# One PSUM bank for each half of the turned weights in the causal stage of a six-layer attention kernel

## The chip, the cores and the metric

The kernel runs on one core of one Trainium2 chip. The metric is the device time of one execution in microseconds, the median of several runs. TensorE (PE) does the matmuls and the transposes through the identity and writes only to PSUM. VectorE (DVE) and ScalarE (ACT) read PSUM and do the arithmetic element by element. GpSimd (POOL) works in SBUF alone here, and SyncE (SP) starts the transfers. PSUM is used as eight banks of 128 x 512 numbers.

## The reference

Input `x` is 8 sequences of 512 tokens with 256 features, all float32. Six layers follow each other, each over all eight sequences: attention "a" (8 heads, low-rank keys and values), two feed-forward layers "f" with local attention, the causal attention "b", and again the two "f" layers with the same weights. What the change touches is "b":

```python
qkv = x @ w_qkv + b_qkv                       # x is layer-normed; 16 heads of 16
dot = jnp.einsum('bhid,bhjd->bhij', q, k)
q_norm_sq = jnp.sum(q * q, axis=-1, keepdims=True)
k_norm_sq = jnp.sum(k * k, axis=-1, keepdims=True)
vals = q_norm_sq + k_norm_sq.transpose(0, 1, 3, 2)
scores = dot * dot / (vals - 2.0 * dot + EPSILON) * SCORE_SCALE
mask = jnp.triu(jnp.ones((Lq, Lq), dtype=scores.dtype), k=1) * -1000000000.0
attn = jax.nn.softmax(scores + mask[None, None, :, :], axis=-1)
out = jnp.einsum('bhij,bhjd->bhid', attn, v)
out = out.transpose(0, 2, 1, 3).reshape(Bq, Lq, E)
return out @ w_out + b_out
```

## The kernel before, in words

Everything stays in SBUF. The work is cut into 48 units `u`: layer `u // 8`, sequence `u % 8`. The causal layer is units 24 to 31. A unit's work is cut into parts, each named by a kind, a unit and an index, and each kind belongs to one engine.

A causal unit has 24 steps: 8 pairs of heads times three groups of rows of the score matrix (`B_TILES`: row tiles 1 and 0, then tile 2, then tile 3, of 128 rows each). Only the blocks at or below the diagonal are computed, 3, 3 or 4 blocks of 128 x 128 for each of the two heads. One step is this chain:

- PE `bden` and `bdot`: the denominator and the dot product, each into a pair of banks (`wide0`, `wide1` or `wide2`, one bank for each head). In the trace they are the matmuls `wide<-hid` and `wide<-x,w_up`, and `bden` ends with `wide<-far_b,ident_b`.
- ACT `bnum` (square of the dot product, L1249) and `bguess` (logarithm and exponential for a first reciprocal, L1260 and L1264).
- DVE `bclose` (L1422) and `bmul` (L1430 and the four or two instructions of L1436): one Newton step for the reciprocal, the scores, and the largest of each row. POOL `neg` changes that to the bias of the exponential (L1655).
- ACT `exp` (L1287).
- PE `turn_a` and `turn_b`: 6 or 8 transposes of 128 x 128 (L896) into PSUM, two to four of them in each half. The halves are called the turned weights here.
- The copies to SBUF: of half a by ACT (`pt_a`, L1294) in the first of three steps and by DVE (`pt_c`, L1471) in the others, and of half b by DVE (`pt_b`), where the blocks on the diagonal are multiplied by the causal mask (L1479) and the rest is copied (L1482).
- PE `mix`: the product with the values, into `o_ps`. After 24 steps follow `sel`, `fan` and the output projection `proj` on PE, with `osum` and `out_b` (L1496) and `res` (L1502) on DVE between and behind them.

The next unit's head of the work (`bqkv` on PE, `row` on DVE at L1409, `bk` and `bq` on PE) is woven between the steps.

Seven of the eight banks are handed out by name; `o_ps` is the eighth. `wide0` to `wide2` are banks 0 to 5 in pairs, and bank 6 is `turn_ps`. In the causal stage before the change, `bk`, `bq`, `sel` and `fan` use bank 6, and the two halves of the turned weights share one pair: half a lies in its first bank, half b in its second. `turn_a` takes the pair, and whoever is given that pair next waits for the copies of both halves.

What sets the order is a planner that runs when the kernel is built. `ordered()` walks through all parts with the durations of `cost()`, and for each engine takes, among the parts that could start no later than `PATIENCE` after the first possible one, the part with the smallest due time. A due time is the part's place in its unit plus an offset from the table `DUE`. `rooms()` says which banks a part may use, `buffer_at()` picks among them the one that is free first by the planner's durations, and `readers_of()` says whose end frees them. The engines then run their lists in that order. Each part waits on semaphores for what it needs; a PE part also waits in `psum_read()` for the readers of the earlier contents of its banks.

Of the kernel before, what the change touches and what calls it, by code (L numbers as in the profile page):

```python
# [13 lines left out]
P = 128  # L14
# [50 lines left out]
B_OWN = [4, 2, 2]  # L65
# [148 lines left out]
def normed_before(u):  # L214
# [244 lines left out]
def holder_of(part):  # L459

    kind, u, i = part
    if kind == "turn_b" and stage_of(u) == "b":
        return ("turn_a", u, i)
    return (kind, u, 0) if kind in ("proj", "down") else part
# [6 lines left out]
def rooms(part):  # L471


    kind, u, i = part
    st = stage_of(u)
    pairs, single = [(f"wide{k}", (2 * k, 2 * k + 1)) for k in range(3)], (f"bank{BANKS - 1}", (BANKS - 1,))
    if st == "a" and kind in ("score", "turn_a", "turn_b"):
        return [single] + [(f"bank{k}", (k,)) for k in range(A_PAIRS * 2, BANKS - 1)]
    if kind in NARROW and not (kind == "turn_a" and st == "b"):
        return [single]  # L480
    return pairs[:A_PAIRS] if st == "a" else pairs


def readers_of(part):

    kind, u, i = part
    last = [(r, u, 0 if kind in ("proj", "down") else i) for r in READERS[kind]]
    if kind == "turn_a" and stage_of(u) == "b":
        last.append(("pt_b", u, i))
    if kind == "score" and stage_of(u) == "f":  # L490
        last.remove(("exp", u, i))
    return last
HOP = 0.2

PATIENCE = 0.263


def ordered():
# [34 lines left out]
    def buffer_at(part):  # L533
# [5 lines left out]
        for name, banks in rooms(part):  # L539
            at = 0.0  # L540
            for holder in {holders[k] for k in banks} - {None}:
                for r in readers_of(holder):
                    if r in parts:
                        at = max(at, end[r] + HOP) if at is not None and r in end else None
            if at is not None and (best is None or at < best[0]):
                best = (at, name)
# [81 lines left out]
def build(nc, d):  # L628
    stack = ExitStack()
    with stack:  # L630
# [128 lines left out]
        def psum_read(pe, part):  # L759
# [36 lines left out]
            elif kind == "turn_a" and stage_of(u) == "b":  # L796
                pe.wait_ge(S[first_copy(u, i)], nth(first_copy(u, i), u, i))
                pe.wait_ge(S["pt_b"], nth("pt_b", u, i))
            elif kind == "turn_a":
                pe.wait_ge(S["pt_a"], nth("pt_a", u, i))  # L800
# [88 lines left out]
        def tensor_program(eng):  # L889
# [9 lines left out]
            for part in ORDER["PE"]:  # L899
# [139 lines left out]
                elif kind in ("turn_a", "turn_b") and stage_of(u) == "b":  # L1039
                    pe.wait_ge(S["exp"], nth("exp", u, i))  # L1040
                    for k, block in B_TURNS[i % 3][kind == "turn_b"]:
                        to, at = turned_to(i, k, block), k * b_width(i) + block * P
# [280 lines left out]
        def vector_program(eng):  # L1323
# [10 lines left out]
            for part in ORDER["DVE"]:  # L1334
# [132 lines left out]
                elif kind == "pt_c":  # L1467
# [3 lines left out]
                    eng.tensor_copy(prob_t[SLOTS[u, i]["pt"]][:, 0:w], wide[PLACE["turn_a", u, i]][:, 0:w]).then_inc(S["pt_c"], 1)  # L1471
                elif kind == "pt_b":
# [3 lines left out]
                    if stage_of(u) == "b":  # L1476
                        dve.wait_ge(S["const"], 16 * 3)
                        ps, met, n = wide[PLACE["turn_b", u, i]], P * B_OWN[i % 3], P * len(B_TURNS[i % 3][1])
                        last = eng.tensor_tensor(blocks(pt[:, 512:512 + met]), blocks(ps[:, 512:512 + met]),  # L1479
                                                 causal_keep[:, :].unsqueeze(1).to_broadcast([P, met // P, P]), ALU.mult)  # L1480
                        if n > met:
                            last = eng.tensor_copy(pt[:, 512 + met:512 + n], ps[:, 512 + met:512 + n])  # L1482
# [395 lines left out]
```

## Time and profile before

| | us |
|---|---|
| median of 3 runs | 4371.79 (4367.45 to 4373.05) |
| profiled execution, time | 4363.23 |
| profiled execution, span | 4361.2 |
| PE busy | 4070.3 (93%) |
| DVE busy | 3157.0 (72%) |
| ACT busy | 2469.0 (57%) |
| causal stage, taken as 1981 to 3010 us | 1029 |
| one causal unit | 133.4 |

Busy time is a share of the span, an average over stages. The table by stretches shows that PE is nearly always busy in the "f" stages and that DVE is the busiest engine in the causal stage. "PEclk" is the share of the full TensorE clock that was granted. Idle time of an instruction stands in brackets with the engine and the line that ended it. "PEld" is the weight load ahead of a matmul, which overlaps the matmul before it.

### The profile page before, as it was taken

To read this page: it belongs to the slowest core of one execution; us is meant where nothing else is said; L and a number is where in the kernel's file an instruction comes from. 1 tells how busy PE (TensorE), PEld (TensorE's weight loads), DVE (VectorE), ACT (ScalarE), POOL (GpSimd) and SP (SyncE) were. 2 spreads that over 40 slices of the span, in tenths; PEclk is the share of its full clock that TensorE was granted. 3 is DMA by queue.
4 is the path that set the end of the run, shared out by engine and by line. 5 is a ranking of instruction groups with operands and counts; after the bars stand their busy time and mean duration, and the time that the engine had idled before them with its cause. 6 is when DMAs were issued, how large, how long until landed. Compare 5 with 4: busy or idle time off the path is not lost.

```text
span 4361.2 us, 66411 instructions
## 1 busy us (share of the span) xinstructions
PE 4070.3 (93%) x23504; PEld 2586.4 (59%) x23504; DVE 3157.0 (72%) x7625; ACT 2469.0 (57%) x5353; POOL 1763.7 (40%) x2051
## 2 busy tenths in 40 slices
PE   8999999999999999988888888888999999999997
PEld 4666556666666666655555555555666666666664
DVE  6667677777667667658988889888777676677663
ACT  5556554454454545439887788875544544544441
POOL 2223365555546556420111110014555565565551
PEclk9999999999999999998998889989999999999999
DMA  2000000000010000000000000101000000100000
GB/s 78 11 16 6 25 11 6 3 3 6 23 30 11 13 8 8 26 19 20 23 23 20 20 24 23 37 20 33 4 6 3 3 26 8 35 15 18 13 20 22
DMA packets 63176, 78.38 MB, mean 18 GB/s; under 512 B 15312, under 2 KB 47616, under 8 KB 62848
## 3 DMA queue, kind: packets, MB, share of 16 engines
q1 hardware_dynamic: 62848, 74.14, 5.9%
q8 instruction: 189, 3.10, 0.3%
q14 instruction: 139, 1.14, 0.1%
HBM read 36.39 MB, written 12.58 MB: 11 GB/s over the span
## 4 chain that ended last, share of the span: by engine, by line
PE 70%; DVE 14%; ACT 10%; issue 5%; DMA 0%; SPq 0%; POOL 0%; DVEq 0%; ACTq 0%
PE wide L893 48%; PE o_ps L893 8%; PE wide L896 7%; PE turn_ps L896 5%; ACT prob L1270 3%; DVE w_up L1422 2%; PE turn_ps L893 2%; DVE prob L1436 1%; DVE hid L1430 1%; ACT prob L1287 1%; DVE turned L1368 1%; ACT x L1260 1%; ACT hid L1260 1%; DVE ss L1375 1%; DVE turned L1382 1%
## 5 line engine op out<-in xcount | busy, mean ns | idle before, releaser
L893 PE MATMUL wide<-x,w_up 128*128 128x512 f32 (+3 forms) x2528 | 837.5, 540 | 4.2 <-DVE x L1533 2.2
L893 PE MATMUL wide<-w_in,x_t 128*128 128x512 f32 (+2 forms) x1920 | 801.4, 561 | 4.6 <-ACT x_t L1183 1.3
L1661 POOL TENSOR_SCALAR prob<-prob,st 128x256 f32<-128x256 f32 (+1 forms) x1024 | 554.4, 560 | 577.2 <-DVE st L1460 576.6
L1270 ACT ACTIVATE prob<-prob,st 128x256 f32<-128x256 f32 (+1 forms) x1024 | 479.5, 470 | 166.9 <-DVE st L1447 166.5
L893 PEld LDWEIGHTS wide<-x,w_up 128*128 128x128 f32 (+2 forms) x2528 | 374.9, 192 | 300.4 <-issue 283.3
L893 PEld LDWEIGHTS wide<-w_in,x_t 128*128 128x128 f32 x1920 | 339.3, 191 | 332.4 <-issue 323.0
L893 PE MATMUL o_ps<-pt,v 128*32 128x128 f32 (+2 forms) x5120 | 485.1, 332 | 37.8 <-DVE pt L1486 30.6
L1633 POOL TENSOR_TENSOR rn<-ss,minus_half 128x16 f32<-128x16 f32 x128 | 433.7, 3389 | 126.2 <-DVE ss L1377 121.9
L893 PEld LDWEIGHTS o_ps<-pt,v 128*64 128x64 f32 (+1 forms) x5120 | 308.2, 128 | 219.4 <-issue 89.7
L1447 DVE CUSTOM_DVE_ANT_0 prob<-wide,local_mask 128x256 f32<-128x256 f32 (+1 forms) x1024 | 335.3, 382 | 140.4 <-PE wide L893 140.4
L1625 POOL TENSOR_TENSOR sines<-raw,rot 128x512 f32<-128x512 f32 x256 | 351.5, 1394 | 196.7 <-ACT raw L1190 196.7
L1298 ACT ACTIVATE o_t<-o_ps 128x512 f32<-128x512 f32 x192 | 113.5, 591 | 490.3 <-PE o_ps L893 490.3
L1655 POOL TENSOR_SCALAR st<-st 128x2 f32<-128x2 f32 (+1 forms) x192 | 39.8, 207 | 858.8 <-DVE st L1436 858.8
L893 PE MATMUL wide<-k_t,q_t 64*128 64x256 f32 (+2 forms) x2450 | 366.4, 411 | 2.2 <-ACT turned L1193 1.2
L893 PE MATMUL wide<-w_out,o_t 128*128 128x256 f32 x1536 | 351.3, 388 | 1.9 <-ACT o_t L1298 1.9
L893 PE MATMUL wide<-hid 18*128 18x256 f32 x992 | 204.1, 507 | 148.9 <-DVE pt L1479 99.5
L893 PE MATMUL wide<-w_down,hid 128*128 128x256 f32 (+1 forms) x1536 | 330.5, 383 | 4.6 <-DVE hid L1556 4.6
L896 PEld LDWEIGHTS turn_ps<-ident,prob 128*128 128x128 f32 x1932 | 230.5, 141 | 175.6 <-issue 139.5
L893 PEld LDWEIGHTS wide<-w_out,o_t 128*128 128x128 f32 x1536 | 298.7, 196 | 58.1 <-issue 14.2
L896 PE MATMUL turn_ps<-ident,prob 128*128 128x128 f32 x1932 | 310.2, 278 | 24.2 <-ACT pt L1294 14.8
L1556 DVE SCALAR_TENSOR_TENSOR hid<-wide,bias_up,hid 128x512 f32<-128x512 f32 (+1 forms) x224 | 144.8, 669 | 241.6 <-ACT hid L1317 122.6
L896 PE MATMUL wide<-ident,prob 128*128 128x128 f32 x1828 | 272.3, 294 | 13.5 <-DVE raw L1409 11.0
(166 smaller groups left out, 7498.9 us busy)
## 6 DMA issues: line engine op xcount, KB each, us to landing
kept<-resid SPq DMA_DIRECT2D x16, 512.0 KB, 2.6
x<-kept SPq DMA_DIRECT2D x16, 512.0 KB, 3.3
w_up<-hid SPq DMA_DIRECT2D x62, 128.0 KB, 2.2
x<-hid SPq DMA_DIRECT2D x62, 128.0 KB, 2.3
shifted<-resid SPq DMA_DIRECT2D x32, 224.0 KB
w_in<-in_f_wqkv SPq DMA_DIRECT2D x4, 1536.0 KB, 6.5
w_up<-in_f_w SPq DMA_DIRECT2D x4, 1492.0 KB, 6.5
resid<-in_x SPq DMA_DIRECT2D x8, 512.0 KB, 7.9
```

What stands on the lines that cost most here:

```text
L893: return eng.matmul(out, lhsT, rhs, start=start, stop=stop, skip_group_check=True)
L896: return eng.transpose(out, in_, ident[:, :])
L1260: last = eng.activation(inv[:, k * w:(k + 1) * w], ps[:, 512 * k:512 * k + w], ACT.Ln, bias=guess_add[s][:, i % 3, h:h + 1])
L1270: last = eng.activation(pr[:, local_span(t)], pr[:, local_span(t)], ACT.Exp, bias=sm[:, t:t + 1], scale=-1.0, accum_out=sm[:, 4 + t:5 + t])
L1287: last = eng.activation(pr[:, side], pr[:, side], ACT.Exp, bias=sm[:, c:c + 1])
L1298: eng.activation(o_t[:, i, :], o_ps[:, :], ACT.Copy).then_inc(S["out"], 1)
L1422: eng.scalar_tensor_tensor(out=two(den, slice(0, w)), in0=two(ps[:, :], slice(0, w)), scalar=DEN_MIN, in1=two(inv, slice(0, w)), op0=ALU.m ...
L1447: eng.tensor_tensor_reduce(pr[:, local_span(t)], ps[:, local_span(t)], local_mask[:, P if t == 0 else 0:256], -1.0, LOW, ALU.add, ALU.min, ...
L1556: last = eng.scalar_tensor_tensor(out=hid[rows, m, cols], in0=ps[rows, 512 * k + cols.start:512 * k + cols.stop], scalar=bias_up[rows, m:m ...
L1625: last = eng.tensor_tensor(halves(sines[(o - 1) % 2][:, side]), halves(r[:, side])[:, :, ::-1, :], rot[:, 2 * z + 1, i, :].rearrange("p (u ...
L1633: eng.tensor_tensor(rn[(o - 1) % 2][:, 0:16], ss[(o - 1) % 2][:, 0, :], minus_half[:, 0:16], ALU.pow).then_inc(S["rn"], 1)
L1661: last = eng.tensor_scalar(pr[:, local_span(t)], pr[:, local_span(t)], sm[:, 8 + t:9 + t], 1.0, ALU.mult, ALU.mult)
```

## The change

In the causal stage each half of the turned weights becomes a tile of its own with a single bank. `rooms()` lists bank 6 first and then banks 5 down to 0, and the planner takes the first that is free. A half's bank is given back by the half's own copy. `buffer_at()` counts a bank as free no earlier than PE itself is, so that among banks that are free by then the first of the list is taken. The transposes of half b are written to columns 0 and up of its bank, and the copies read from there. Since `bk`, `bq`, `sel` and `fan` still use bank 6 alone, they now share it with the halves. No instruction is added or removed.

The offsets of the causal kinds in `DUE` are other numbers, and `PATIENCE` goes from 0.263 to 0.318. The table holds only offsets of the due times; two of its lines stand here. `PATIENCE` applies to all stages.

```diff
-    ("b", "turn_a"): -0.01, ("b", "pt_c"): -0.015, ("b", "mix"): 0.031, ("b", "sel"): 0.017, ("b", "osum"): 0.179,
+    ("b", "pt_c"): -0.012, ("b", "mix"): 0.031, ("b", "sel"): 0.017, ("b", "bn_h"): 0.005, ("b", "turn_b"): -0.12,
...
@@ holder_of(part)
     kind, u, i = part
-    if kind == "turn_b" and stage_of(u) == "b":
-        return ("turn_a", u, i)
     return (kind, u, 0) if kind in ("proj", "down") else part
@@ rooms(part)
-    if kind in NARROW and not (kind == "turn_a" and st == "b"):
+    if st == "b" and kind in ("turn_a", "turn_b"):
+        return [single] + [(f"bank{k}", (k,)) for k in reversed(range(BANKS - 1))]
+    if kind in NARROW:
         return [single]
@@ readers_of(part)
-    if kind == "turn_a" and stage_of(u) == "b":
-        last.append(("pt_b", u, i))
...
-PATIENCE = 0.263
+PATIENCE = 0.318
@@ buffer_at(part)
+            if at is not None and stage_of(u) == "b":
+                at = max(at, free_at["PE"])
@@ psum_read(pe, part)
-            elif kind == "turn_a" and stage_of(u) == "b":
+            elif kind == "turn_a":
                 pe.wait_ge(S[first_copy(u, i)], nth(first_copy(u, i), u, i))
-                pe.wait_ge(S["pt_b"], nth("pt_b", u, i))
-            elif kind == "turn_a":
-                pe.wait_ge(S["pt_a"], nth("pt_a", u, i))
@@ tensor_program
-                        to, at = turned_to(i, k, block), k * b_width(i) + block * P
+                        to, at = turned_to(i, k, block) % 512, k * b_width(i) + block * P
@@ vector_program, pt_b
-                        ps, met, n = wide[PLACE["turn_b", u, i]], P * B_OWN[i % 3], P * len(B_TURNS[i % 3][1])
+                        ps, met, n = buffers[PLACE["turn_b", u, i]], P * B_OWN[i % 3], P * len(B_TURNS[i % 3][1])
-                        last = eng.tensor_tensor(blocks(pt[:, 512:512 + met]), blocks(ps[:, 512:512 + met]),
+                        last = eng.tensor_tensor(blocks(pt[:, 512:512 + met]), blocks(ps[:, 0:met]),
```

Below, `wide0` to `wide2` are the pairs and `turn_ps` is bank 6. The first place is on PE at the seam of two causal units, units 27 and 28, where step 0 of unit 28 is done and step 1 follows. `wide<-w_in,x_t` is the next unit's `bqkv`, `<-ident,prob1` x6 are the halves of step 21 of unit 27, `<-ident,k_t0` is `bk`, and `<-hid`, `<-x_2,w_up` and `<-far_b` are step 1's `bden` and `bdot`. Before:

```order
L893 MATMUL wide1<-w_in,x_t 128x512
L893 MATMUL wide1<-w_in,x_t 128x256
L896 MATMUL wide0<-ident,prob1 128x128 x6
L896 MATMUL turn_ps<-ident,k_t0 128x128 x4
L893 MATMUL wide1<-hid 128x384 x2
L893 MATMUL wide0<-x_2,w_up 128x384 x2
L893 MATMUL wide1<-far_b,ident_b 128x128 x2
L896 MATMUL wide2<-ident,prob2 128x128 x6
```

After, from the turning of half b of step 21 (`prob1`, four blocks) through step 0's `bden` and `bdot` (256 and 128 columns), half a of step 21 (two blocks), the halves of step 22 (`prob2`) and step 1's `bden` and `bdot` (384 columns):

```order
L896 MATMUL turn_ps<-ident,prob1 128x128 x4
L893 MATMUL wide1<-hid 128x256 x2
L893 MATMUL wide2<-x_2,w_up 128x256 x2
L893 MATMUL wide1<-hid 128x128 x2
L893 MATMUL wide2<-x_2,w_up 128x128 x2
L893 MATMUL wide1<-far_b,ident_b 128x256 x2
L896 MATMUL turn_ps<-ident,prob1 128x128 x2
L893 MATMUL o_ps<-pt0,v1 32x128 x8
L896 MATMUL wide2<-ident,prob2 128x128 x2
L896 MATMUL turn_ps<-ident,prob2 128x128 x4
L893 MATMUL wide0<-hid 128x384 x2
L893 MATMUL wide2<-x_2,w_up 128x384 x2
```

Step 1's `bdot` took the pair that both halves of step 21 had just filled; now step 21's halves lie in bank 6, one after the other, and step 1's `bden` and `bdot` take pairs 0 and 2, where pair 2 holds only half b of step 22. `bqkv` stands further ahead and no longer before these rows.

The second place is on PE at the head of unit 28. `<-w_in,x_t` is the second `bqkv` of unit 29, `turn_ps<-o_t,w_down` is `sel`, `<-ident,prob1` is step 1 turned, and the 384 columns are step 4. Before:

```order
L893 MATMUL wide1<-w_in,x_t 128x512
L893 MATMUL wide1<-w_in,x_t 128x256
L893 MATMUL turn_ps<-o_t,w_down 32x512 x4
L893 MATMUL wide0<-hid 128x384 x2
L893 MATMUL wide2<-x_2,w_up 128x384 x2
L893 MATMUL wide0<-far_b,ident_b 128x128 x2
L896 MATMUL wide1<-ident,prob1 128x128 x6
```

After:

```order
L893 MATMUL wide2<-hid 128x384 x2
L893 MATMUL wide0<-x_2,w_up 128x384 x2
L893 MATMUL wide2<-far_b,ident_b 128x128 x2
L893 MATMUL turn_ps<-o_t,w_down 32x512 x4
L896 MATMUL wide0<-ident,prob1 128x128 x2
L893 MATMUL wide1<-w_in,x_t 128x512
L893 MATMUL wide1<-w_in,x_t 128x256
...
L896 MATMUL wide2<-ident,prob1 128x128 x4
```

Before, the halves of step 1 went into pair 1 right where `bqkv` had been; now half b goes ahead of `bqkv`, half a behind it, and both into banks that `bqkv` does not hold.

The third place is on DVE at the same seam. L1341, L1345 and L1328 are the layer norm statistics of a later unit, L1409 is `row`, L1479 with 512 columns is `pt_b` of step 21, and L1422 is `bclose`. Before:

```order
L1436 ISA st3 128x1
L1341 BN_STATS stat_h<-resid 128x6 x4
L1345 BN_AGGR stat_h<-stat_h 128x2 x4
L1328 TENSOR_SCALAR stat_h<-stat_h 128x4
L1409 TENSOR_TENSOR raw0<-wide1,w_in 128x768
L1479 TENSOR_TENSOR pt1<-wide0,causal_keep 128x512
L1422 SCALAR_TENSOR_TENSOR w_up<-wide2,x_2 128x768
```

After:

```order
L1479 TENSOR_TENSOR pt1<-turn_ps,causal_keep 128x256
L1409 TENSOR_TENSOR raw0<-wide2,w_in 128x768
L1471 COPY pt1<-wide1 128x512
L1471 COPY pt0<-turn_ps 128x512
L1479 TENSOR_TENSOR pt0<-wide1,causal_keep 128x256
L1482 COPY pt0<-wide1 128x256
L1341 BN_STATS stat_h<-resid 128x6 x4
L1345 BN_AGGR stat_h<-stat_h 128x2 x4
L1328 TENSOR_SCALAR stat_h<-stat_h 128x4
L1479 TENSOR_TENSOR pt1<-turn_ps,causal_keep 128x512
L1422 SCALAR_TENSOR_TENSOR w_up<-wide0,hid 128x1024
```

The statistics still stand right before `pt_b` of step 21, but `row` and the copies of steps 19 and 20 stand before them, and `bclose` and `bmul` of step 23 (prob3, 512 columns for each head) now come behind that copy.

## Rows read from the trace of the kernel before

**Rows 1.** The page: span, and busy time, share and instructions of each engine.
```profile
span 4361.2 us, 66411 instructions
PE 4070.3 (93%) x23504; PEld 2586.4 (59%) x23504; DVE 3157.0 (72%) x7625; ACT 2469.0 (57%) x5353; POOL 1763.7 (40%) x2051
```

**Rows 2.** Busy time by stretches: eight "f" units, then the causal stage.
```profile
core 0: us, PE busy (x) PEld busy (x) DVE busy (x) ACT busy (x) POOL busy (x), PEclk, DMA share, GB/s
646.00:1312.00 666.00, 657.24 (x3268) 420.43 (x3266) 467.55 (x1217) 325.11 (x777) 371.34 (x377) 1.00 0.04 12
1981.00:3010.00 1029.00, 855.45 (x7042) 550.24 (x7040) 901.63 (x1955) 851.27 (x1493) 131.69 (x349) 0.90 0.09 22
```

**Rows 3.** The same for two causal units.
```profile
2216.00:2349.40 133.40, 111.55 (x905) 71.90 (x905) 115.40 (x252) 108.99 (x194) 14.44 (x47) 0.88 0.08 21
2349.40:2482.80 133.40, 111.52 (x905) 71.76 (x905) 115.42 (x252) 108.89 (x194) 14.46 (x47) 0.88 0.08 21
```

**Rows 4.** Groups of the causal stage, 1981 to 3010 us; last, idle before and releaser.
```profile
L893 PE MATMUL wide<-hid 18*128 18x256 f32 x976 | 198.7, 502 | 148.8 <-DVE pt L1479 99.5 <-DVE pt L1482 27.1 <-DVE pt L1471 9.3
L1249 ACT ACTIVATE prob<-wide 128x768 f32<-128x768 f32 x183 | 159.9, 874 | 89.6 <-PE wide L893 78.5 <-remote 9.0
L1422 DVE SCALAR_TENSOR_TENSOR w_up<-wide,x 128x768 f32<-128x768 f32 x122 | 116.0, 951 | 13.6 <-ACT x L1264 12.1
L1471 DVE COPY pt<-wide 128x512 f32<-128x512 f32 x125 | 85.7, 686 | 13.9 <-PE wide L896 13.9
L1422 DVE SCALAR_TENSOR_TENSOR w_up<-wide,hid 128x1024 f32<-128x1024 f32 x62 | 75.7, 1221 | 22.2 <-ACT hid L1264 22.2
L1496 DVE TENSOR_TENSOR o_t<-turn_ps,o_t 128x512 f32<-128x512 f32 x29 | 20.0, 691 | 31.6 <-PE turn_ps L893 31.6
```

**Rows 5.** PE at the seam of units 27 and 28, in order of time.
```profile
2440.54 0.60 PE L896 MATMUL turn_ps<-ident,k_t 128*128 128x128 f32 x4
2444.47 1.01 PE L893 MATMUL wide<-hid 18*128 18x384 f32 x2 [3.33 <-DVE pt L1479]
```

**Rows 6.** DVE and ACT at the same seam, in order of time.
```profile
2443.64 0.68 DVE L1479 TENSOR_TENSOR pt<-wide,causal_keep 128x512 f32<-128x512 f32 x1
2448.85 0.96 DVE L1422 SCALAR_TENSOR_TENSOR w_up<-wide,x 128x768 f32<-128x768 f32 x1 [0.48 <-ACT x L1264]
2452.06 0.69 DVE L1471 COPY pt<-wide 128x512 f32<-128x512 f32 x1 [0.18 <-PE wide L896]
2454.74 1.22 DVE L1422 SCALAR_TENSOR_TENSOR w_up<-wide,hid 128x1024 f32<-128x1024 f32 x1 [1.33 <-ACT hid L1264]
...
2446.19 0.81 ACT L1249 ACTIVATE prob<-wide 128x768 f32<-128x768 f32 x1 [2.90 <-PE wide L893]
```

**Rows 7.** PE at the head of unit 28, in order of time.
```profile
2461.26 0.29 PE L893 MATMUL wide<-far_b,ident_b 128*128 128x128 bf16 x2
2463.66 1.06 PE L896 MATMUL wide<-ident,prob 128*128 128x128 f32 x6 [2.11 <-DVE raw L1409]
```

**Rows 8.** Busy time by stretches around that wait, and one unit earlier.
```profile
2463.00:2464.00 1.00, 0.34 (x3) 0.34 (x4) 1.00 (x2) 0.97 (x3) 0.01 (x1) 1.00 0.00 0
2464.00:2485.00 21.00, 21.00 (x86) 11.77 (x85) 12.76 (x22) 10.13 (x18) 1.74 (x7) 0.51 0.06 13
2331.00:2352.00 21.00, 21.00 (x85) 11.88 (x84) 12.93 (x23) 9.86 (x18) 1.74 (x7) 0.51 0.06 13
```

**Rows 9.** An "f" unit: PE in order of time, then ACT.
```profile
921.94 8.75 PE L893 MATMUL wide<-x,w_up 128*128 128x512 f32 x20
930.52 0.49 PE L896 MATMUL turn_ps<-ident,prob 128*128 128x128 f32 x3
977.81 1.74 PE L893 MATMUL o_ps<-pt,v 128*64 128x256 f32 x16 [1.10 <-DVE pt L1486]
...
926.22 0.19 ACT L1270 ACTIVATION_READ_ACCUMULATOR prob<-prob,st 128x1 f32 x1
931.92 0.60 ACT L1202 ACTIVATE q_t<-wide 128x512 f32<-128x512 f32 x1 [5.51 <-PE wide L896]
```

More of the change, by code:

```diff
@@ L1470, in vector_program @@
                     w = P * len(B_TURNS[i % 3][0])
-                    eng.tensor_copy(prob_t[SLOTS[u, i]["pt"]][:, 0:w], wide[PLACE["turn_a", u, i]][:, 0:w]).then_inc(S["pt_c"], 1)
+                    eng.tensor_copy(prob_t[SLOTS[u, i]["pt"]][:, 0:w], buffers[PLACE["turn_a", u, i]][:, 0:w]).then_inc(S["pt_c"], 1)
                 elif kind == "pt_b":
@@ L1477, in vector_program @@
                         dve.wait_ge(S["const"], 16 * 3)
-                        ps, met, n = wide[PLACE["turn_b", u, i]], P * B_OWN[i % 3], P * len(B_TURNS[i % 3][1])
-                        last = eng.tensor_tensor(blocks(pt[:, 512:512 + met]), blocks(ps[:, 512:512 + met]),
+                        ps, met, n = buffers[PLACE["turn_b", u, i]], P * B_OWN[i % 3], P * len(B_TURNS[i % 3][1])
+                        last = eng.tensor_tensor(blocks(pt[:, 512:512 + met]), blocks(ps[:, 0:met]),
                                                  causal_keep[:, :].unsqueeze(1).to_broadcast([P, met // P, P]), ALU.mult)
                         if n > met:
-                            last = eng.tensor_copy(pt[:, 512 + met:512 + n], ps[:, 512 + met:512 + n])
+                            last = eng.tensor_copy(pt[:, 512 + met:512 + n], ps[:, met:n])
                         last.then_inc(S["pt_b"], 1)
```

15 rows, old and new, of the table DUE are left out of this document.

## The prediction

> **What bounds the kernel now.** I read the busy times of the page first. They show PE at 93% of the span and DVE at 72% [rows 1], which would make PE the bound everywhere. So I read the table by stretches next, since the change touches one stage. The "f" units run at the full clock with PE busy 657.24 of 666 us: there PE is the bound. The causal stage is another matter. PE is busy 855.45 of 1029 us, ACT 851.27 and DVE 901.63, and the granted clock is 0.90 [rows 2]. No engine is full. A causal unit takes 133.4 us, and DVE works 115.4 of them [rows 3]. The reader is to see two numbers in this: the stage cannot fall below DVE's 115.4 us for each unit, and there are 18.0 us for each unit, or 1029 - 901.63 = 127 us in the stage, in which DVE is idle. Whatever this change gains must come out of those 127 us, since it removes no instruction.
>
> Third, I read the groups of the causal stage. PE waits 99.5 + 27.1 + 9.3 = 135.9 us in front of `bden` and `bdot` for copies of turned weights, which is the wait that the change works on. But PE is not what bounds the stage. The wait matters only where DVE or ACT starve behind it. ACT waits 78.5 us for PE's dot products in front of L1249. DVE waits 13.9 us for turned weights at L1471, 12.1 + 22.2 us for ACT's guess at L1422, and 31.6 us for `fan` at L1496 [rows 4]. So 136 us of waiting on PE stand against idle pieces on DVE that are much smaller and have several causes.
>
> Fourth, I read the order of time at one seam of two units, to see which idle pieces hang on a pair of banks.
>
> At the first place PE ends `bk` at 2441.1 and starts step 1 at 2444.47, after 3.33 us of waiting for `pt_b` [rows 5]. That copy is behind the statistics and `row` in DVE's list and starts at 2443.64. PE's wait starves ACT, which idles 2.90 us in front of step 1's square. DVE itself is busy with the statistics all that time and pays later, with 0.48 + 0.18 + 1.33 = 1.99 us of idle time [rows 6].
>
> At the second place, the head of the unit, PE waits 2.11 us for `row` [rows 7], because the turned weights of step 1 go into the pair that `bqkv` holds. Then something larger follows. The clock, 1.00 in the microsecond of that wait, is at half for almost all of the next 21 us, with PE busy 21.00 of them. DVE works only 12.76 us in that stretch, so 8.24 us of its 18 idle us in the unit lie there. One unit earlier it is the same: 21 us, 12.93 us of DVE [rows 8]. In other words PE, at 1.2 GHz instead of 2.4, is the bound for 21 us in each unit, and what came just before was a pause of PE.
>
> **The change part by part.** I sum against the profiled execution, 4363.2 us with a span of 4361.2. It lies 8.6 us under the median of the runs, 4371.8, and I move the result by that at the end.
>
> *Instructions.* The same transposes, copies and matmuls are issued, with the same widths. 0 us.
>
> *The wait at the seam.* Step 1's `bdot` no longer takes the pair of the half that has just been turned. In the new order it takes pair 2, which holds `pt_b` of step 22's half instead, and step 21's copy only frees bank 6. So part of the wait goes away and part is replaced by a copy that stands elsewhere in DVE's list. The statistics still stand in front of `pt_b` of step 21, but `row` no longer stands between them and the copy, and `bclose` and `bmul` of step 23 have moved behind it. What DVE gets back is bounded by 1.99 us above [rows 6]. Below it is bounded by minus the wait of PE, 3.33 us [rows 5], should the new order put such a wait in a place where DVE has nothing to do. I take 1.99, as the order names a free pair for `bden` and a different copy for `bdot`. There are 7 seams inside the stage: 7 x 1.99 = 14 us.
>
> *The wait for `row`.* Half b of step 1 is turned before `bqkv` and half a behind it, into bank 5. The wait for `row` is then gone at that place; what is late next is `bclose` of step 4, which frees pair 2. PE has `bqkv` to do meanwhile. The wait itself cost DVE nothing at once (DVE is busy 1.00 of 1.00 in rows 8). Its price is the half clock behind it: between 0 and 8.24 us for each unit [rows 8]. Below zero the bound is the same 8.24 with the other sign, for one more such stretch. I take a quarter, 2.06 us, because `sel`, `fan`, `proj` and the small matmuls are still packed there and other pauses of PE of that size stay nearby: 7 x 2.06 = 14 us. Both ends stay in the range: 0 to 58 us.
>
> *The steady part between.* In the rest of the unit DVE is idle 18.0 - 1.99 - 8.24 = 7.8 us, mostly in front of L1422 and L1471, about 0.3 us for each step. Before, a pair was held until both copies were done; now the pair of one half is free after one copy, and bank 6 carries the other. That helps. But the list now bunches things: `exp` runs two steps behind the squares more often, and several copies stand together on DVE. DVE gains at most its 7.8 us and loses what PE may wait at one place, 3.33 us, in a unit. I take 0, with -7.8 to +3.3 for each unit kept.
>
> *Bank 6 is shared.* `bk`, `bq`, `sel` and `fan` now wait for a copy of turned weights too, where a half lay in the bank before them. The copies are 0.69 us (L1471 in rows 4). If each of the four `fan` were behind one such copy, it would be 4 x 0.69 = 2.8 us for each unit, 19 us in all. `fan` is on DVE's own chain (31.6 us at L1496, rows 4). In the order nothing is turned into bank 6 between the four `fan` of the unit that I read, so I take 0 and keep 0 to +19.
>
> *The new `PATIENCE` in the other stages.* In each "f" unit `turn_a` and `turn_b` of step 2 move behind two other groups, and `pt_a` of that step moves behind an `exp`. ACT ends that `exp` at 926.4 and then idles 5.51 us until 931.92, and PE would now issue that `turn_a` at about 930.5, so the copy falls into idle time of ACT [rows 9]. PE's only idle time in the unit, 1.10 us, is in front of another step's `mix` [rows 9]. 0 us, with 0.3 us to either side for 32 units: -10 to +10.
>
> *Sum.* -14 - 14 = -28 us against 4363.2, that is 4335.2, and moved by 8.6 us to the median: 4344 us, or 0.64% faster. What a measurement of this kernel can tell from no change is about 0.2%, 8.7 us.
>
> The clock also speaks for itself against this change. As told, PE at half clock costs DVE 8.24 us in one stretch [rows 8]. The Trainium skill, page "TensorE: Matmul & The Clock Gate", section "A second HAM failure mode: psum-queue depth-cycling", says that small idle pieces of PE between groups of matmuls that cycle through PSUM banks can make the clock swing between its two levels. By this rule a finer cycling, seven single banks in place of three pairs, would swing it more often, and my sum would come out as the third rival below. The trace agrees that the clock swings in this stage (0.90, against 1.00 in the "f" stretch of rows 2), not that finer cycling is worse.
>
> **The rivals.**
>
> *First, nothing gained.* DVE and ACT are near full outside the slow-clock stretch, and PE just waits for other things: for `bclose` instead of `pt_b`. For it: 136 us of waits on PE have only small idle pieces on DVE behind them [rows 4]. Against it: the 2.90 us of ACT and 1.99 us of DVE at the seam have no other cause. Time: 4372 us.
>
> *Second, the long slow-clock stretch goes.* If with the wait for `row` the pause of PE before 2464 goes and none takes its place, DVE regains all 8.24 us in 7 units: 58 us, plus 14 from the seam, 72 us. Time 4300 us. For it: the stretch is the same in both units read. Against it: PE is idle 22 us of a unit, and at a DVE-bound pace this idle time has to be somewhere.
>
> *Third, slower: the clock falls more often.* Because the new list bunches `exp` and copies, PE gets its idle time in longer pieces, and a pause of over 2 us opens in a place where before was none. Each such pause brings a half-clock stretch with 8.24 us of lost DVE time [rows 8]. One more in each unit costs 58 us against the seam's 14: 4372 + 44 = 4416 us. It decides from the second extra stretch in the stage on, since 14 us of gain pay for 1.7 of them; with three or four it is 4385. For it: the pauses of 3.33 and 2.11 us [rows 5, 7] arose from the place of one copy or one `row` in DVE's list, and that list is now another one. Against it: shorter holds of banks give PE more choice, not less.
>
> **How the numbers follow.** My forecast, a gain of 10 to 50 us, has a chance of 0.47. Nothing gained has 0.20, the second rival 0.16, the third 0.17. Faster by over 0.2%: 0.47 + 0.16 = 0.63; within 0.2%: 0.20; slower: 0.17. The likeliest case by itself runs from 4322 to 4362. The range that should hold 8 in 10 reaches from the second rival's 4300 to the beginning of the third, 4380.
>
> **What would show it.** Right: the causal stage shorter by about 28 us with DVE's busy time unchanged at some 902 us; no wait of 3.3 us on L1479 at the seams; the waits for L1409 at the heads gone; PE's waits on L1479, L1482 and L1471 well below 136 us; "f" stretches unchanged at 666 us for eight units. Wrong on the clock: the stage's granted clock clearly above 0.90 (second rival) or below it (third). Wrong on the order: waits in front of L1496 above 31.6 us, which would be the shared bank 6, or "f" stretches that differ by more than 2 us for eight units.

## The result, and the profile after

| | before | after |
|---|---|---|
| median, us | 4369.62 (4 runs) | 4343.86 (4 runs) |
| profiled execution, time, us | 4363.23 | 4345.66 |
| ratio of the runs | | 0.9932 (0.9914 to 0.9949) |
| ratio, second chip, 5 rounds | | 0.9959 (0.9945 to 0.9973) |

The kernel became faster by 0.4 to 0.7%. One of the four runs after took 13,904.75 us, and one of `e7_fill_4` below 9433.55 us; these rare executions are counted in the medians of the tables (without them the medians are 4342.06 and 4323.54) and left out of the ratios. The forecast was 4344 us. That the number fits is partly luck, as the steps below show.

First, the page after. The columns are those of [rows 1].

```profile
span 4343.5 us, 66308 instructions
PE 4079.8 (94%) x23504; PEld 2583.5 (59%) x23504; DVE 3157.0 (73%) x7625; ACT 2474.4 (57%) x5353; POOL 1767.2 (41%) x2051
```

DVE has the same 3157.0 us of work, so no time came from less work. Next, where the 17.6 us between the two profiled executions lie. I took the start of each unit's last addition on DVE (L1502, `res`, in all units, and L1565, `res2`, in "f" units) from the trace in order of time and compared the two kernels:

| stretch | before, us | after, us | difference |
|---|---|---|---|
| start to `res2` of unit 23 | 1943.58 | 1948.85 | +5.3 |
| from there to the first `res` behind the causal stage | 1140.2 | 1110.6 | -29.6 |
| from there to the last `res2` | 1272.8 | 1279.5 | +6.6 |
| one "a" unit | 64.99 | 65.28 | +0.29 |
| one "f" unit (mean over 13) | 83.60 | 83.93 | +0.33 |

In this pair of traces the causal stage gained 29.6 us and the other stages lost 12. The second stretch takes in the ends of the causal stage, which overlap its neighbours. Its length differs between executions of one kernel: in the trace of `again`, the changed kernel once more, it took 1118.4 us, which is a gain of 21.8. Here are the stretches, answering to [rows 2] and [rows 3]: eight "f" units, the causal stage, and three causal units, each from one `res` to the next.

```profile
core 0: us, PE busy (x) PEld busy (x) DVE busy (x) ACT busy (x) POOL busy (x), PEclk, DMA share, GB/s
646.00:1312.00 666.00, 656.54 (x3262) 419.80 (x3261) 466.32 (x1215) 326.55 (x776) 366.51 (x374) 1.00 0.04 11
1981.00:2990.00 1009.00, 873.09 (x7087) 549.53 (x7086) 904.66 (x1994) 861.62 (x1523) 143.34 (x356) 0.91 0.09 23
2106.29:2228.20 121.91, 105.71 (x906) 67.48 (x904) 113.35 (x252) 108.80 (x192) 15.61 (x47) 0.94 0.09 23
2228.20:2353.11 124.91, 108.51 (x906) 68.87 (x904) 113.39 (x253) 109.35 (x194) 15.60 (x47) 0.92 0.09 22
2353.11:2479.07 125.96, 108.53 (x906) 69.59 (x904) 113.53 (x252) 108.98 (x192) 15.60 (x47) 0.92 0.09 22
```

And the same cut, from `res` to `res`, through the kernel before, for units 25 to 29. These rows were not shown ahead of the prediction, and they matter:

```profile
2097.52:2224.21 126.69, 103.76 (x908) 68.04 (x908) 114.91 (x252) 108.96 (x192) 14.46 (x47) 0.95 0.09 22
2224.21:2357.48 133.27, 111.42 (x908) 71.84 (x909) 115.39 (x252) 108.97 (x192) 14.44 (x47) 0.88 0.08 21
2357.48:2490.74 133.26, 111.38 (x908) 71.63 (x908) 115.42 (x252) 108.75 (x193) 14.46 (x47) 0.88 0.08 21
2490.74:2624.00 133.26, 111.20 (x908) 71.59 (x908) 116.14 (x252) 108.76 (x193) 18.14 (x51) 0.88 0.10 25
2624.00:2749.73 125.73, 104.09 (x908) 67.80 (x908) 113.84 (x252) 109.31 (x194) 12.09 (x46) 0.95 0.09 22
```

The order of the instructions on each engine is the same in these five units of before (only the pairs of banks alternate from unit to unit, also among the three of 133.3 us). Three take 133.3 us at a clock of 0.88 and two take about 126 us at 0.95. One order has two speeds, and the clock goes with them. The prediction had looked at two of the 133.3 us kind and taken 133.4 us for all.

The groups that answer to [rows 4], from the causal stage after, 1981 to 2990 us. "turn_ps" is bank 6.

```profile
L893 PE MATMUL wide<-hid 18*128 18x512 f32 x980 | 195.1, 495 | 49.0 <-issue 17.4 <-ACT pt L1294 11.1 <-DVE w_up L1422 6.4
L1249 ACT ACTIVATE prob<-wide 128x1024 f32<-128x1024 f32 x184 | 160.8, 874 | 68.5 <-PE wide L893 67.9
L896 PE MATMUL wide<-ident,prob 128*128 128x128 f32 x706 | 118.5, 297 | 31.8 <-ACT prob L1287 13.1 <-DVE pt L1471 9.3 <-ACT prob L1249 4.6
L896 PE MATMUL turn_ps<-ident,prob 128*128 128x128 f32 x548 | 97.0, 293 | 19.3 <-DVE pt L1479 11.0 <-ACT prob L1287 7.6 <-ACT pt L1294 0.2
L896 PE MATMUL turn_ps<-ident,q_t 128*128 128x128 f32 x116 | 18.9, 287 | 11.6 <-DVE pt L1471 6.9 <-DVE pt L1479 2.9 <-DVE pt L1482 1.3
L1471 DVE COPY pt<-wide 128x512 f32<-128x512 f32 x86 | 58.9, 684 | 6.8 <-PE wide L896 6.6
L1496 DVE TENSOR_TENSOR o_t<-turn_ps,o_t 128x512 f32<-128x512 f32 x31 | 21.4, 690 | 12.3 <-PE turn_ps L893 11.6
```

And the group of the turning before, which [rows 4] does not show:

```profile
L896 PE MATMUL wide<-ident,prob 128*128 128x128 f32 x1245 | 192.9, 300 | 12.4 <-DVE raw L1409 11.0 <-ACT turned L1193 0.8 <-ACT prob L1249 0.2
```

In front of `bden` and `bdot` PE now idles 49.0 us in place of 148.8. In front of the turning it idles 31.8 + 19.3 = 51.1 us in place of 12.4, partly for `exp` (L1287), which was not among the causes before. ACT starves 68.5 us in place of 89.6, and DVE 12.3 in place of 31.6 us for `fan`.

The seam and the head of unit 28 after, PE in order of time, only rows with a wait that the text speaks of, as in [rows 5] and [rows 7], and then the clock at this head:

```profile
2441.97 0.63 PE L896 MATMUL turn_ps<-ident,q_t 128*128 128x128 f32 x4 [1.25 <-DVE pt L1471]
2452.41 0.59 PE L893 MATMUL wide<-hid 18*128 18x384 f32 x2 [1.74 <-ACT pt L1294]
```

```profile
2464.00:2485.00 21.00, 20.98 (x148) 14.68 (x144) 15.75 (x31) 13.18 (x24) 1.83 (x8) 0.92 0.07 27
```

The pause of 3.33 us has become smaller ones, the wait for `row` is gone, and where 21 us at half clock had stood [rows 8], the granted clock is 0.92. Not all pauses became short: in the middle of units 27 to 29 one of 2.06 to 2.07 us stands in front of `bden`, for which the profile shows no cause ("issue").

To compare units I use "low-clock time" below: the granted clock of each microsecond of a stretch, summed as 2 x (1 - granted).

| units 25 to 29, from `res` to `res` | us | low-clock time, us |
|---|---|---|
| before | 126.7, 133.3, 133.3, 133.3, 125.7 | 14, 31, 31, 31, 14 |
| after | 121.9, 124.9, 126.0, 123.2, 126.0 | 14, 20, 20, 14, 20 |

### The profile page after: what moved, and what is told of

Read it like the earlier page. It is cut to its first block, busy times and chain, and to the rows that moved or that the text cites. A ratio compares the mean times of both kernels' runs of the same rounds, so it can differ in the third digit from the quotient of the medians.

```text
span 4343.5 us, 66308 instructions
## 1 busy us (share of the span) xinstructions
PE 4079.8 (94%) x23504; PEld 2583.5 (59%) x23504; DVE 3157.0 (73%) x7625; ACT 2474.4 (57%) x5353; POOL 1767.2 (41%) x2051
## 4 chain that ended last, share of the span: by engine, by line
PE 70%; DVE 16%; ACT 8%; issue 5%; POOL 0%; DMA 0%; SPq 0%; ACTq 0%; DVEq 0%
PE wide L893 48%; PE o_ps L893 8%; PE wide L896 6%; PE turn_ps L896 5%; ACT prob L1270 3%; PE turn_ps L893 2%; DVE prob L1436 2%; DVE turned L1368 1%; DVE ss L1375 1%; DVE w_up L1422 1%; DVE prob L1447 1%; DVE x L1430 1%; DVE turned L1382 1%; DVE x L1533 1%; ACT x L1260 1%
## 5 line engine op out<-in xcount | busy, mean ns | idle before, releaser
L896 PE MATMUL turn_ps<-ident,prob 128*128 128x128 f32 x2500 | 411.0, 282 | 47.6 <-ACT pt L1294 18.2
L896 PEld LDWEIGHTS turn_ps<-ident,prob 128*128 128x128 f32 x2500 | 300.1, 143 | 230.4 <-issue 166.8
L1294 ACT ACTIVATE pt<-turn_ps 128x512 f32<-128x512 f32 (+1 forms) x294 | 170.1, 579 | 239.2 <-PE turn_ps L896 238.9
L893 PEld LDWEIGHTS wide<-w_down,hid 128*128 128x128 f32 (+1 forms) x1536 | 255.8, 189 | 44.4 <-issue 10.6
L1486 DVE COPY pt<-turn_ps 128x384 f32<-128x384 f32 (+1 forms) x266 | 148.3, 558 | 172.8 <-PE turn_ps L896 172.2
```

Of the source, the lines that this page charges most:

```text
L893: return eng.matmul(out, lhsT, rhs, start=start, stop=stop, skip_group_check=True)
L896: return eng.transpose(out, in_, ident[:, :])
L1294: eng.activation(pt[:, 0:w], buffers[PLACE["turn_a", u, i]][:, 0:w], ACT.Copy).then_inc(S["pt_a"], 1)
L1486: eng.tensor_copy(pt[:, 512:512 + w], buffers[PLACE["turn_b", u, i]][:, 0:w]).then_inc(S["pt_b"], 1)
```

## The experiments

The medians stand against the kernel before on the same chip. Those that shared a chip: the first four; `e5_not_bank6` and `e6_wait_row`; the four from `e1_again` on; the last two.

| run | median, us | ratio to before, 95% |
|---|---|---|
| again | 4347.50 | 0.9959 (0.9945 to 0.9973) |
| e1_patience_b | 4339.92 | 0.9941 (0.9926 to 0.9957) |
| e2_banks_alone | 4398.03 | 1.0073 (1.0059 to 1.0088) |
| e3_table_alone | 4397.60 | 1.0074 (1.0059 to 1.0089) |
| e5_not_bank6 | 4405.24 | 1.0093 (1.0078 to 1.0108) |
| e6_wait_row | 4385.12 | 1.0059 (1.0036 to 1.0083) |
| e1_again | 4334.93 | 0.9935 (0.9922 to 0.9947) |
| e4b_both_copies | 4370.28 | 1.0016 (1.0005 to 1.0027) |
| e7_fill_4 | 4326.85 | 0.9904 (0.9889 to 0.9918) |
| e8_fill_8 | 4333.95 | 0.9933 (0.9921 to 0.9945) |
| e7b_fill_4 | 4329.92 | 0.9913 (0.9899 to 0.9927) |
| e9_fill_before | 4362.96 | 0.9993 (0.9983 to 1.0003) |

### The change again, and the other stages

> The changed kernel once more, on the same chip as the three below, so that they can be compared with it. Expected: 4344 us (0.993 of the kernel before), with units 25 to 29 about 125 us apart (133.3 before), the "f" units 83.6 us apart (83.27 before).

The time was 4347.50, and units 25 to 29 took 127.0, 126.0, 124.3, 124.8 and 124.4 us, with the same low-clock time as after, 18 us on average. The "f" units were 83.92 us apart; the "83.27 before" of the expectation is the period within one layer, and the mean that includes the step between layers is 83.60.

```diff
-PATIENCE = 0.318
+PATIENCE = {"a": 0.263, "f": 0.263, "b": 0.318}
...
-                best = min((a for a in able if a[0] <= first + PATIENCE), key=lambda a: a[1])
+                patience = PATIENCE[stage_of(min(able)[2][1])]
+                best = min((a for a in able if a[0] <= first + patience), key=lambda a: a[1])
```

> The changed kernel with PATIENCE 0.318 for the causal stage alone and 0.263 for the others as before; outside the causal stage the order is that of before but for a few parts at its end. Theory (the other stages pay 0.32 us for each "f" unit and 0.2 for each "a" unit for the new PATIENCE): the "f" units go back to 83.27 us, 30 units and 6 "a" units give back 11 to 13 us, total 4331. Rival (the 0.32 us are the run's or the chip's, not the order's): "f" units stay at 83.6 and the time at 4344.

The "f" units went back to 83.60 us and the "a" units to 64.99. The time was 4339.92 beside 4347.50, 7.6 us less, where 11 to 13 were expected. The intervals of the two ratios overlap, so the medians alone don't show it, but the periods of the units hardly vary. In the profiled execution the start was 2.9 us and the end 3.7 us shorter than in `again`, and the units that overlap the causal stage kept another order than before. `e1_again` gave 4334.93. All traces together say the same: the stretch up to `res2` of unit 23 took 1944.2 us on average in the seven traces with the old PATIENCE in these stages and 1948.7 in the six with the new one, and the stretch from the first `res` behind the causal stage to the last `res2` took 1274.8 against 1278.7. So the new PATIENCE costs the other stages about 8 us. A part of it shows in the changed kernel as a new wait of PE, here from the waits in the stretch of the eight "f" units:

```profile
PE wide L893 <- DVE x L1533: 1.5, 7, 0.2
PEld turn_ps L896 <- POOL prob L1661: 1.7, 7, 0.2
```

The columns are the total, the times and the longest. In seven of the eight units `up_g` waits 0.2 us for the copy of the transposed `x`, since `turn_a` of step 2, which had stood between, is now behind `up_g`. The turning's first weight load waits 0.2 us too. Neither row is in the kernel before.

### Banks and table apart

`e2_banks_alone` is the changed kernel with the offsets and the PATIENCE of before, and `e3_table_alone` is the kernel before with the new offsets and PATIENCE.

> The single banks, each given back by its own copy, with the offsets and the PATIENCE of before, so the planner orders the causal stage for the new banks with the old table. Theory A (the banks make the gain): the pauses of PE before the row wait and at the seams shrink already, causal units about 127 us, total about 4325 to 4335 since the "f" units keep 83.27 us. Theory B (banks and table belong together, the order must be fitted to the banks): causal units 131 to 137 us, total 4360 to 4400.

> The new offsets and PATIENCE with the old shared pairs. Theory A (the banks make the gain): causal units stay at 133 us or become longer, plus 10 us in the "f" stages, total 4380 or more. Rival (the order makes the gain, the banks are incidental): causal units 125 to 128 us, total 4345 to 4360.

Both came out slower than before by 0.7%. Units 25 to 29 took 136.4, 135.6, 134.6, 141.2, 127.8 us with the banks alone, and 136.5, 136.5, 132.8, 131.2, 131.4 with the table alone. Theory A of the first run, that the banks by themselves make the gain, fell, and so did the rival of the second, that the order by itself makes it. Banks and order make the gain together. Low-clock time in these units was 33 and 35 us on average, against 24 before and 18 after.

### The seventh bank

```diff
-        return [single] + [(f"bank{k}", (k,)) for k in reversed(range(BANKS - 1))]
+        return [(f"bank{k}", (k,)) for k in reversed(range(BANKS - 1))]
```

> The halves go into the six banks of the pairs only, not into bank 6; offsets and PATIENCE of the changed kernel, the planner orders anew. Theory (the seventh bank is what leaves a pair free for the next scores): the waits of PE for a pair come back, causal units 131 us or more, total 4385 or more. Rival (the own copy is enough): units at most 127 us, total up to 4360. The new order is not fitted to this case, so that only a small loss would be clear evidence.

The time was 4405.24: above 4385, as the theory expected, with units of 128.7, 139.6, 133.0, 133.2, 133.0 us. PE's waits in front of `bden` and `bdot` came back:

```profile
L893 PE MATMUL wide<-hid 18*128 18x384 f32 (+3 forms) x952 | 202.9, 525 | 96.1 <-ACT pt L1294 27.6 <-DVE pt L1471 25.5 <-DVE pt L1482 17.3
```

That is 96.1 us against 49.0 with bank 6. But the table was not searched for six banks, and `e2_banks_alone` shows what an unfitted table alone can cost, so how much of the 58 us is the bank's stays open.

### Giving back by the own copy

```diff
                 for held in HELD.get(part, ()):
                     psum_read(pe, held)
+                    other = other_copy(held, part)
+                    if other is not None:
+                        pe.wait_ge(S[other[0]], nth(*other))
```

`other_copy` names the copy of the other half where the planner had placed it before the part that waits.

> The changed kernel in its own order and with its own places, but before PE reuses a half's bank it also waits for the other half's copy, in 305 of 384 holds (in the other 79 that would lock up). Theory (giving back by the own copy is a part of the gain): causal units 2 us or more longer than the 124 to 126 of the changed kernel, total 4360 or more. Rival (the seventh bank and the fitted order make the gain): units within 1 us of 125, total 4344 to 4352.

Order and places are those of the changed kernel, so this one is clean of the table. The time was 4370.28 (ratio 1.0016), by the ratios 25 to 37 us more than the changed kernel, with units of 132.0, 129.8, 129.8, 126.9, 124.5 us. Nothing of the gain is left, though only 305 of the 384 holds have the wait. So the gain needs the own copy, in this order at least. Low-clock time in these units was 27 us on average in place of 18, which suggests that a part of what the own copy is worth comes by way of the clock. A version with the wait in 369 holds, `e4_both_copies`, locks up and has no time.

### The pause and the clock

```diff
                 elif kind == "bdot":
                     g, half = i // 6, i // 3 % 2
+                    if i == 5 and 26 <= u <= 30:
+                        pe.wait_ge(S["row"], nth("row", u + 1, 1))
```

> The changed kernel with one wait more in five units: step 5's scores on PE wait for the second row of the next unit, as step 1's turning did before. It makes PE pause by about 2 to 2.5 us at the place where the long half-clock stretch began before. Theory (the pause brings the 21 us at half clock, and these cost DVE 8 us): a long stretch of low clock at these five heads, units 7 to 9 us longer, total about 4380. Rival (the stretch came from the kind of work there, and the wait costs itself alone): no low-clock stretch over 8 us, units 1 to 2.5 us longer, total 4350 to 4356.

The time was 4385.12, 38 us above `again` (44 by the ratios). PE's added pause is the same at all five heads, 1.55 us where 2 to 2.5 had been expected; here the first, third and fourth in order of time, and then three stretches of 22 us behind them:

```profile
2216.86 0.70 PE L893 MATMUL wide<-hid 18*128 18x512 f32 x2 [1.55 <-DVE raw L1411]
2479.05 0.70 PE L893 MATMUL wide<-hid 18*128 18x512 f32 x2 [1.55 <-DVE raw L1411]
2606.07 0.70 PE L893 MATMUL wide<-hid 18*128 18x512 f32 x2 [1.55 <-DVE raw L1411]
```

```profile
2218.00:2240.00 22.00, 22.00 (x86) 13.64 (x87) 12.76 (x29) 8.64 (x14) 2.13 (x9) 0.53 0.06 13
2481.00:2503.00 22.00, 21.98 (x149) 15.26 (x148) 15.55 (x30) 13.20 (x23) 2.06 (x9) 0.92 0.11 37
2607.00:2629.00 22.00, 22.00 (x89) 13.46 (x86) 12.97 (x29) 8.46 (x13) 2.05 (x9) 0.53 0.05 12
```

And the five units, from `res` to `res`:

```profile
2108.21:2243.66 135.45, 116.83 (x906) 73.25 (x904) 113.69 (x252) 109.14 (x192) 15.53 (x47) 0.86 0.08 21
2243.66:2373.24 129.58, 112.00 (x906) 72.12 (x904) 113.59 (x252) 108.90 (x192) 15.53 (x47) 0.89 0.09 22
2373.24:2497.90 124.66, 107.09 (x906) 69.17 (x904) 113.69 (x253) 108.71 (x192) 15.51 (x47) 0.93 0.09 22
2497.90:2632.88 134.98, 116.34 (x906) 74.27 (x904) 114.49 (x253) 109.48 (x193) 19.29 (x51) 0.86 0.10 25
2632.88:2765.83 132.95, 115.37 (x906) 73.20 (x904) 113.71 (x252) 109.03 (x192) 13.16 (x46) 0.87 0.08 21
```

One pause of 1.55 us in one and the same order: in three units the long half-clock stretch follows and they take 133 to 135 us, in one it is shorter (129.6), and in one it does not come, and that unit takes 124.7 us, as long as without the wait (124.3 in `again`). So the wait costs nothing that can be seen by itself; with the long stretch behind it the units are 8 to 11 us longer than that one. In the two traces of the changed kernel without the wait, no half-clock stretch at these five heads is longer than 7 us. My theory had the mechanism right and expected it at all five heads. That it does not come each time is what the two 126 us units of the kernel before show as well.

### Filling PE's pauses

```diff
                 elif kind == "bden":
-                    continue
+                    for _ in range(2):
+                        for k in range(2):
+                            mm(ps[:, 512 * k:512 * k + 2 * P], ident_b[:, :], far_b[:, :, :], True, True)
```

This is on the kernel of `e1_patience_b`; `range(4)` makes the 8 extra matmuls, and `e9_fill_before` puts the 4 into the kernel before.

> The kernel of e1_patience_b with 4 extra bf16 matmuls of 256 columns in each causal step, into the pair that bden has just been given, ahead of the wait for bdot's pair: what they write is overwritten. They fill PE's pauses with about 0.45 us in each of 192 steps, 86 us of PE work where PE is idle about 150. Theory (pauses of PE let the clock fall, and the half clock costs DVE time): the low-clock time of the causal stage falls from about 205 us to under 150 and the time by 5 to 15 us, to 4325 to 4335. Rival (PE's work is on the path wherever the clock is low or the head of a unit is): 4350 to 4400.

> The same with 8 extra matmuls for each step, about 0.9 us in each of 192 steps, 170 us in all, more than PE's idle time. Theory of the clock: low-clock time below 100 us, but PE becomes the bound; the time is 4340 to 4400, and the loss is smaller than the 170 us added by at least half. Rival (clock not helped): the loss is 60 us or more over e7_fill_4 and the low-clock time stays near 200 us.

> The kernel of e7_fill_4 once more, since the profiled execution there was one of the rare ones that take twice as long. Expected: 4327 us again; low-clock time of the causal stage between the 41 us with 8 extra matmuls and the 208 us with none; causal units 123 to 125 us.

> The kernel before, with shared pairs, old offsets and old PATIENCE, and the same 4 extra matmuls in each causal step. Theory (half or more of what separates the kernels in the steady units is the long half-clock stretch at the head, which costs DVE 8.2 us): the stretch of 21 us goes, the three equal units of 133.3 us fall to 126 or less, total 4320 to 4345. Rival (the pairs themselves hold the units at 133 us): units stay above 130, total 4355 or more. In between, 4345 to 4355 with units of 127 to 130 us, both have a part.

The stage without extra matmuls (`e1_again`), then with 4 (`e7b_fill_4`) and with 8 (`e8_fill_8`):

```profile
1981.00:2990.00 1009.00, 867.15 (x7057) 547.49 (x7057) 896.33 (x1962) 851.72 (x1499) 136.97 (x350) 0.91 0.09 23
```

```profile
1981.00:2990.00 1009.00, 913.62 (x7850) 587.43 (x7851) 911.64 (x1994) 860.43 (x1521) 150.39 (x364) 0.97 0.09 24
```

```profile
1981.00:2990.00 1009.00, 956.17 (x8511) 643.00 (x8510) 901.20 (x1979) 857.63 (x1512) 144.21 (x358) 0.98 0.09 23
```

The same of the kernel before, then with 4 (`e9_fill_before`):

```profile
1981.00:2990.00 1009.00, 837.04 (x6925) 540.39 (x6924) 889.19 (x1923) 840.23 (x1468) 119.27 (x336) 0.90 0.09 23
```

```profile
1981.00:2990.00 1009.00, 901.73 (x7664) 587.96 (x7663) 888.51 (x1925) 843.30 (x1470) 119.49 (x337) 0.93 0.09 23
```

Low-clock time from 1940 to 3020 us fell from 208 us (`e1_again`) to 85 with 4 and to 41 with 8. With 4, the ratios are 0.9904 and 0.9913 where `e1_again` has 0.9935, which is 10 to 14 us less, and units 25 to 29 took 122.5, 123.2, 124.0, 122.6, 122.0 us. With 8, the clock stays up nearly always, the five units take 125.2, 125.0, 125.0, 125.0, 124.9, and the time is that of `e1_again`. The likely reason is that more PE work takes away what the clock gives; no run shows the two parts by themselves. The one with 4 is the fastest version found: single banks, PATIENCE by stage and 4 extra matmuls, where the change alone has 0.9932 and 0.9959.

In the kernel before, the 4 extra matmuls changed the time by nothing (0.9983 to 1.0003). The three units of 133.3 us fell to 132.1, 130.7, 132.1 and the other two rose, from 126.7 to 130.6 and from 125.7 to 126.4. That is the rival's outcome, and it speaks against a fixed price of the slow clock: low-clock time from 1940 to 3020 us fell from 222 to 157 us, and DVE's idle time in the same 1080 us stayed at 140.0. Two effects may be mixed in it: the stretch at the head went down to 14 us and less, and the extra work stands ahead of `bdot` in units whose PE already waits there for the pair. No run tells them apart.

## Why the prediction was right, and where not

**That the gain comes out of DVE's idle time in the causal stage: right.** DVE's work is unchanged at 3157.0 us. DVE's idle time in one unit was 17.1 to 17.9 us in the 133.3 us units of before and is 8.6 to 12.4 us after. The stretch of the causal stage became 29.6 us shorter in one pair of traces and 21.8 with the trace of `again`, where 28 had been forecast.

**The seam, 1.99 us: about right in size.** It can be read where the low-clock time is equal, 14 us. DVE is idle 11.8 and 11.9 us in those units of before and 8.6 and 9.1 after, 3.0 us less, with units of 126.7 and 125.7 against 121.9 and 123.2, 3.7 us less. The 1.99 us of the seam and the 0 us of the steady part together stand against these 3.0 to 3.7. `e4b_both_copies` shows that the own copy is needed for the gain; it does not show how much of these 3.0 to 3.7 us it gives.

**The wait for `row` and the slow clock, a quarter of 8.24 us at 7 heads: mis-sized twice.** The price of one stretch was about right: 133.3 - 126.2 = 7.1 us in the kernel before, and 8 to 11 us in `e6_wait_row`. But of the five steady units, 25 to 29, it came in three and not in all, and the change removed it from all three, not from a quarter. The mean low-clock time of the five fell from 24 to 18 us. With 7.1 us of unit for 17 us of low-clock time that is about 2.6 us for each of them. This is an estimate, and `e9_fill_before`, where low-clock time fell without a gain, says that the rate is not a constant. My step "PE is the bound for 21 us in each unit" failed, since I had read the two neighbouring units of [rows 3], both with the stretch, and not those without it.

So the five steady units gained 6.0 us each (130.4 to 124.4): by this estimate 2.6 from the clock and 3.4 from banks and order. My terms had been 2.06 and 1.99. In the other traces with the same order of these units they averaged 125.3 (`again`) and 126.0 us (`e1_patience_b`, `e1_again`), a gain of 5.1 and 4.4, so each part is good to about 1 us.

**The first rival's and third rival's grounds.** Waits did move to the turning (51.1 us in place of 12.4), but not one for one with the 99.8 us that went away in front of `bden` and `bdot`. The clock did fall more often, as the third rival said, 35 times in place of 26 from 1940 to 3020 us. But the stretches were shorter: low-clock time went from 222 to 202 us, and DVE's idle time inside them from 47 to 25 us. The rule of the Trainium skill, page "TensorE: Matmul & The Clock Gate", section "A second HAM failure mode: psum-queue depth-cycling", that small idle pieces between groups make the clock swing, is seen here in both kernels: the granted clock of the stage is 0.90 and 0.91, no idle time of PE in it is longer than 3.33 us, and with 4 matmuls in each step to fill the pauses it is 0.97 in the kernel of `e7b_fill_4`. Whether finer cycling of banks makes it worse, these runs leave open: with single banks low-clock time was 202 us in the fitted order and 270 in the old one (`e2_banks_alone`), and with pairs 222 in the old order and 273 in the new one (`e3_table_alone`). The order changed with the banks each time.

**The shared bank 6, 0 us: right by its sign.** The wait at L1496, the sign named for it, fell from 31.6 to 12.3 us. PE does wait for the bank elsewhere: in front of `bq` it idles 11.6 us in place of 1.0, mostly for the copies of halves, and the 1.25 us at 2441.97 above is one such wait. What that costs no run shows.

**PATIENCE elsewhere, 0 us: wrong by 12 us in the profiled execution, 8 us over all traces.** I bounded it at 0.3 us for each "f" unit to either side and took the middle. It was 0.33, just beyond that range, which makes 2.6 us in eight "f" units and so the sign that I had named (more than 2 us). The "a" units, which I had not priced at all, lost 0.29 us each. I had checked the copy on ACT, but not what was left without cover when the turning moved: `up_g`, right behind the transposes of `x`, waits for their copy.

Added up for the profiled execution: -29.6 in the causal stage against my -28, and +12 against 0. The 4344 fits because the runs of the first comparison moved by 26 us, more than the 17.6 of the profiled executions and the 18.5 of the second chip; against those it would have been 9 to 10 us too low. That much is luck. Where and how long the half-clock stretches come differs between executions of one kernel, and that may be why the medians do; no run here tells it apart.

## What to carry to other kernels

Before a unit is taken as typical, cut all repetitions at the same instruction and put time and granted clock side by side: one order had two speeds here, 126 and 133 us. In a stage where VectorE is the busiest engine, a pause of TensorE can still cost time, because of the slow clock behind it; cheap matmuls whose result is overwritten, placed ahead of a wait, gave 10 to 14 us with single banks and nothing in the kernel before, so such a filler has to be measured in each order. And a planner's constant that was changed for one stage should be kept to that stage: a gain of 22 to 30 us came with a loss of 8 to 12 us that nobody had asked for.

## What was not expected of the hardware

- The same pause of 1.55 us of PE, in the same order, was followed by 22 us at a granted clock of 0.53 in three cases of five, by 0.69 in one and by 0.92 in another. The pause was less than half of the 3.33 us of [rows 5], and PE's rows cover 86 to 87% of these units.
- Half clock did not end with the pause that came before it: from 2464 to 2485 us of the kernel before, PE was busy 21.00 of 21 us at a granted clock of 0.51 [rows 8].
- PE busy (its rows overlap) went up with the filler from 867 to 914 and 956 us in the stage of 1009 us, while the kernel got 10 to 14 us faster with 4 extra matmuls and stayed equal with 8.
